# w1 and w2 laid out by 32x32 squares, so that VectorE instead of TensorE transposes them, in a fused kernel of attention approximation and NF4 feed-forward

## The chip, the cores and the metric

The kernel runs on one core of a Trainium2 chip. The metric is the device time of one execution in microseconds (us). The kernel before takes 429.08 us, the median of three runs (428.99 to 429.38).

## What is computed

For 1024 tokens x of width 512 the reference computes two layers. Each adds its result to x and normalises over the 512 features:

```
up = x @ up_w.T;  delta = x @ gate_w.T - local_point            # width 128
approx = sum over m = 0..6 of (term_m(delta) * up) @ W_m.T        # seven 128 -> 512 products
ffn1 = (silu(x @ ffn_gate_w.T) * (x @ ffn_up_w.T)) @ ffn_down_w.T # hidden width 1248
x = layernorm(x + approx + ffn1)
dq = nf4_quant_dequant(w)   # per 64 elements: a = max|w|; nearest of 16 codes to w/a; times a
ffn2 = (silu(x @ dq(w1).T) * (x @ dq(w2).T)) @ dq(w3).T           # hidden width 1376
x = layernorm(x + ffn2)
```

w1 and w2 are 1376 x 512 and w3 is 512 x 1376. All is float32.

## The kernel before, in words

**Products.** Each float32 product is three float32r matmuls over a high and a low part: `product()` issues hi·hi, lo·hi and hi·lo (L1144, L1145, L1146). The high part is a rounding copy made by ScalarE (`copy`, L557), the low part a subtraction on VectorE or GpSimd. So each operand passes through two engines before TensorE can read it.

**Stages on TensorE.** In order: `up` and `delta`; 20 pairs of the first layer's hidden projection; passes 0 and 1 of the first output stage (one for each half of the tokens); 22 pairs of the second layer's projection (`pair(2, i)`, 24 matmuls each, for hidden chunk f of 128 and one half of the tokens); passes 2 and 3 of the second output stage. The second layer's projection for chunk f needs the dequantised rows f of w1 and w2 with the contracted feature on the partitions. They come with the hidden row on the partitions, so `transpose_nf4(f)` turns them: eight 128x128 transposes (L1258) of the tile `Q` into PSUM banks 4 and 5. Two calls stand in pass 1 (f = 0, 1), one behind pair 2 and one behind each second pair after it (f = 2 to 10). ScalarE then copies both banks into one of two slots of `w_hi` (`split_nf4`), and VectorE subtracts into `w_lo` (`lo_nf4`, L915). `transpose_x` (L1244) and `transpose_w3` (L1269) do the same for x and w3 and stay.

**The NF4 work.** It runs beside all this on the other three engines, in 17 units: 0 to 10 are chunks of w1 and w2 (in the tile `Q`, 128 x 1024; unit 10 is 96 x 1024), 11 to 16 are thirds of w3 (in the tile `raw`, 128 x 896, the last ones 128 x 1024 in two parts). For a unit, VectorE takes the block maxima `amax` (L775), keeps them off zero and takes the reciprocal `rcp` (L781, L785), all three in `scales(u)`; GpSimd multiplies by `rcp` (L1060). Then come eight steps k: ScalarE draws a line through the unit and rounds it into an int8 tile `side` (L577 for k = 0, L557 after), GpSimd clamps that into a `level` (L1069, not for k = 0), and VectorE adds the level to a running sum in PSUM banks 6 and 7 (L796 for k = 1, L800 after). After k = 7 VectorE multiplies the sum by `amax` back into the unit (L807), and the unit is dequantised. There are four `side` and three `level` buffers, so GpSimd runs at most three levels ahead of VectorE's additions.

**What sets the order.** Every engine has one fixed program, written by hand. The NF4 steps stand in it where `beside()` is called: the table `SHARE` says for each call of each engine how many steps to take there. `SCALES_AHEAD` and `NORMALISE_AHEAD` put the scales and the multiplication a few steps ahead of a unit's first. Of the semaphores, `s_dq` counts dequantised units, `s_tr` transposed chunks, `s_wlo4` finished low parts. The two transposes of w3 behind the last pair (`transpose_w3(2)` and `(3)`) go into banks 6 and 7 and so wait for the last unit, 16.

**Elsewhere on GpSimd.** In passes 0 and 1 it makes the low parts of hidden activations (`l_lo`, L1099) and of the raw output weights (L1088), and in the second projection the product of gate and up (`h`, L1106), once for each pair.

Of the kernel before, what the change touches and what calls it, by code (L numbers as in the profile page):

```python
# [22 lines left out]
F32 = mybir.dt.float32  # L23
# [93 lines left out]

def unit_rows(u):
    return min(P, F2 - u * P) if u < C2 else P
# [12 lines left out]
def unit_width(u):  # L132
    return UW if u < C2 or is_last_third(u) else 2 * NARROW * BLOCK
# [13 lines left out]
def units_ahead(s, ahead):  # L147
    return [u for u in range(UNITS) if max(0, NB * u - ahead) == s]

# [59 lines left out]
def multiplied(i, pool):  # L209
# [20 lines left out]
    "gpsimd": [  # L230
# [15 lines left out]
def build(nc, xT, xN, w_pre, w_fuse, w_in, w_out, point, discount, w1, w2, w3, ident_in, out):  # L246
    with ExitStack() as ctx:
# [15 lines left out]
        amax, rcp = sb("amax", [P, 4, UW // BLOCK]), sb("rcp", [P, 2, UW // BLOCK])  # L263
# [17 lines left out]
        up2 = Q[:, 0, :].rearrange("p (i n) -> p i n", i=2)  # L281

# [36 lines left out]
        s_line0 = sem("s_line0")  # L319
        s_zero, s_warm = sem("s_zero"), sem("s_warm")  # L320
# [23 lines left out]
        s_xtr, s_tr, s_w3tr = sem("s_xtr"), sem("s_tr"), sem("s_w3tr")  # L344
        s_prep, s_nrm = sem("s_prep"), sem("s_nrm")
# [87 lines left out]
        NF4_BANK = 4  # L433
# [9 lines left out]
        def scaled(u):  # L443
            return 3 * unit_count(u)
# [6 lines left out]
        def unit_read(u):  # L451
            if u < C2:
                return Q[0:unit_rows(u), u, :]
# [8 lines left out]
        def unit_parts(u):  # L462
            p = unit_rows(u)
            if u < C2:
                return [(Q[0:p, u, :].rearrange("p (b e) -> p b e", e=BLOCK), 0, UW // BLOCK)]
# [8 lines left out]
        def per_block(t, u, b, n):  # L474
            v = t[0:unit_rows(u), u % t.shape[1], b:b + n]
            return v.rearrange("p (r b) -> p r b", r=2) if n == 2 * NARROW else v
# [16 lines left out]
        def _(sp):  # L493
# [13 lines left out]
            def load_unit(u):  # L507
                p = unit_rows(u)
                sp.dma_start(Q[0:p, u, 0:D], w1[u * P:u * P + p, :]).then_inc(s_q[u], 16)
                sp.dma_start(Q[0:p, u, D:2 * D], w2[u * P:u * P + p, :]).then_inc(s_q[u], 16)  # L510
# [44 lines left out]
        def _(act):  # L555
# [58 lines left out]
            def silu(layer, i):  # L614
# [8 lines left out]
                if layer == 2 and on_pool(i):  # L623
                    k = multiplied(i, True) - 1
                    if k == 0:

                        act.wait_ge(s_tr, 1)
                    elif k >= 2:
                        act.wait_ge(s_h2, k - 1)
# [16 lines left out]
            def split_x(t):  # L646
# [4 lines left out]
                else:  # L651
                    act.wait_ge(s_tile, TT)
                copy(x_hi[:, :, t * P:(t + 1) * P],
                     PS[:, NF4_BANK + t % 2, :].rearrange("p (c t) -> p c t", c=DC)).then_inc(s_xh, 1)

            def split_nf4(f):
                beside()
                m = rows(f, F2)
                act.wait_ge(s_tr, f + 1)
                wait_nf4_slot(act, f)  # L660
                copy(in_slot(w_hi, f, 2 * DC * m).rearrange("p (c m) -> p c m", m=m),
                     PS[:, NF4_BANK:NF4_BANK + 2, :].rearrange("p b (c m) -> p (b c) m", m=P)[:, :, 0:m]
                     ).then_inc(s_whi4, 1)
# [92 lines left out]
        def _(dve):  # L756
# [8 lines left out]
            def scales(u):  # L765
                p, done = unit_rows(u), scaled(u - 1)
                if u < C2:
                    dve.wait_ge(s_q[u], 32)
                else:
                    dve.wait_ge(s_w3[w3_place(u)[0]], 16)  # L770
                parts = unit_parts(u)
                if u >= 4:
                    dve.wait_ge(s_dq, quantised(u - 4))
                for blocks, b, n in parts:
                    v.tensor_reduce(per_block(amax, u, b, n), blocks, AX_X, ALU.max,  # L775
                                    apply_absolute_value=True).then_inc(s_prep, 1)
                if u >= 2:
                    dve.wait_ge(s_nrm, normalised(u - 2))
                for i, (_, b, n) in enumerate(parts):
                    dve.wait_ge(s_prep, done + i + 1)  # L780
                    v.tensor_scalar(rcp[0:p, u % 2, b:b + n], amax[0:p, u % 4, b:b + n], TINY, None,  # L781
                                    ALU.max).then_inc(s_prep, 1)
# [597 lines left out]
```

## Time and profile before

| what | value |
|---|---|
| median of three runs | 429.08 us |
| the profiled execution's own time | 429.23 us |
| its span, first to last instruction | 427.4 us |
| mean granted TensorE clock | 0.994 of full speed |
| TensorE (PE) busy | 417.5 us, 98% |
| VectorE (DVE) busy | 307.1 us, 72% |
| GpSimd (POOL) busy | 293.0 us, 69% |
| ScalarE (ACT) busy | 265.2 us, 62% |

The profile comes from one execution. A start is given in us from the start of the span. Matmuls are pipelined, so the distance between two starts, not the duration of one, is what a matmul costs the queue. Behind each group of instructions stands in brackets the idle time of its engine before it and what ended that. A share of busy time is an average over stages that have different limits.

### The profile page before, as it was taken

How to read it: one execution, taken by the hardware profiler on the slowest of the kernel's cores; microseconds unless marked ns; L12 is line 12 of the kernel's file. 1: busy time of each engine (PE TensorE's matmuls, PEld its weight loads, DVE VectorE, ACT ScalarE, POOL GpSimd, SP SyncE). 2: the span in 40 equal slices, each digit the busy share in tenths (PEclk: the TensorE clock that was granted, in tenths of full speed). 3: DMA queues.
4: the chain of work that ended last, by engine and by line, in shares of the span. 5: the costliest groups of instructions: out<-in, count | busy, mean ns of one | idle time of the engine just before them, and what ended most of it. 6: DMA issues, size and time to landing. Idle time of an engine off the chain costs nothing.

```text
span 427.4 us, 5638 instructions
## 1 busy us (share of the span) xinstructions
PE 417.5 (98%) x1908; PEld 342.9 (80%) x1908; DVE 307.1 (72%) x379; ACT 265.2 (62%) x356; POOL 293.0 (69%) x230
## 2 busy tenths in 40 slices
PE   8999999999999999999999999999999999999992
PEld 6888888888878888888878888888888877888881
DVE  3639989979879966978358889978699974216025
ACT  5576776677668554638837797788677864332612
POOL 0079999888784698248943788899989993444330
PEclk9999999999999999999999999999999999999997
DMA  8994110000013442020060000000000000000202
GB/s 266 399 352 157 51 38 25 26 25 26 25 49 107 145 141 72 0 100 1 0 265 1 2 0 2 0 2 0 2 2 0 2 0 0 2 0 2 98 0 99
DMA packets 10876, 26.51 MB, mean 62 GB/s; under 512 B 1472, under 2 KB 1728, under 8 KB 10336
## 3 DMA queue, kind: packets, MB, share of 16 engines
q1 hardware_dynamic: 10848, 26.16, 17.8%
q8 instruction: 15, 0.25, 0.2%
q14 instruction: 13, 0.11, 0.1%
HBM read 24.06 MB, written 2.10 MB: 61 GB/s over the span
## 4 chain that ended last, share of the span: by engine, by line
PE 88%; ACT 3%; DVE 3%; issue 2%; POOL 2%; DMA 1%; SPq 0%; ACTq 0%; POOLq 0%
PE PS L1144 28%; PE PS L1145 28%; PE PS L1146 28%; PE PS L1258 2%; DMA h<-xT 1%; PE PS L1269 1%; ACT x_hi L557 1%; ACT l_hi L557 1%; POOL x_lo L1088 1%; POOL l_lo L1099 1%; DVE std L894 1%; DVE stats L875 0%; ACT R L643 0%; DVE R L870 0%; PE PS L1244 0%
## 5 line engine op out<-in xcount | busy, mean ns | idle before, releaser
L1069 POOL TENSOR_SCALAR level<-side 128x1024 f32<-128x1024 int8 (+2 forms) x119 | 133.0, 1118 | 13.7 <-ACT side L557 4.1
L1144 PE MATMUL PS<-x_hi,w_hi 128*128 128x512 f32 (+1 forms) x352 | 138.4, 393 | 0.3 <-DVE x_lo L944 0.3
L1146 PE MATMUL PS<-x_hi,w_lo 128*128 128x512 f32 (+1 forms) x352 | 137.2, 390 | 0.0
L1145 PE MATMUL PS<-x_lo,w_hi 128*128 128x512 f32 (+1 forms) x352 | 137.1, 390 | 0.0
L800 DVE TENSOR_TENSOR PS<-PS,level 128x1024 f32<-128x1024 f32 (+2 forms) x102 | 121.8, 1194 | 19.6 <-POOL level L1069 15.1
L557 ACT ACTIVATE side<-Q 128x1024 int8<-128x1024 f32 (+1 forms) x77 | 77.5, 1050 | 16.9 <-DVE PS L796 11.0
L1099 POOL TENSOR_TENSOR l_lo<-h,l_hi 128x512 fp32r<-128x512 f32 (+1 forms) x42 | 55.9, 1337 | 46.4 <-ACT l_hi L557 45.9
L1144 PEld LDWEIGHTS PS<-x_hi,w_hi 128*128 128x128 f32 (+1 forms) x352 | 65.2, 185 | 15.0 <-issue 0.7
L1146 PEld LDWEIGHTS PS<-x_hi,w_lo 128*128 128x128 f32 (+1 forms) x352 | 65.2, 185 | 14.8
L1145 PEld LDWEIGHTS PS<-x_lo,w_hi 128*128 128x128 f32 (+1 forms) x352 | 65.3, 185 | 14.2
L1144 PE MATMUL PS<-x_hi,l_hi 128*128 128x512 f32 x144 | 56.8, 394 | 0.6 <-POOL l_lo L1099 0.6
L1146 PE MATMUL PS<-x_hi,l_lo 128*128 128x512 f32 x144 | 56.2, 390 | 0.0
L1145 PE MATMUL PS<-x_lo,l_hi 128*128 128x512 f32 x144 | 56.1, 390 | 0.0
L622 ACT ACTIVATE h<-PS 128x512 f32<-128x512 f32 (+1 forms) x42 | 25.0, 595 | 41.8 <-PE PS L1146 41.5
L1088 POOL TENSOR_TENSOR w_lo<-raw,w_hi 128x1024 fp32r<-128x1024 f32 (+2 forms) x15 | 31.3, 2090 | 23.6 <-ACT w_hi L557 23.0
L557 ACT ACTIVATE l_hi<-h 128x512 fp32r<-128x512 f32 (+1 forms) x42 | 25.9, 625 | 26.0 <-PE PS L1146 26.0
L557 ACT ACTIVATE side<-raw 128x896 int8<-128x896 f32 (+1 forms) x42 | 38.8, 986 | 3.9 <-DVE PS L796 3.7
L1106 POOL TENSOR_TENSOR h<-h,Q 128x512 f32<-128x512 f32 (+1 forms) x22 | 30.0, 1368 | 6.9 <-ACT Q L557 4.5
L1060 POOL TENSOR_TENSOR Q<-Q,rcp 128x1024 f32<-128x1024 f32 (+1 forms) x11 | 21.0, 1905 | 17.2 <-DVE rcp L785 17.1
L1144 PEld LDWEIGHTS PS<-x_hi,l_hi 128*128 128x128 f32 x144 | 27.1, 188 | 6.2 <-issue 0.8
L1146 PEld LDWEIGHTS PS<-x_hi,l_lo 128*128 128x128 f32 x144 | 27.0, 188 | 5.7
L1144 PE MATMUL PS<-w_hi,l_hi 128*128 128x512 f32 (+1 forms) x80 | 31.6, 395 | 0.0
(77 smaller groups left out, 518.9 us busy)
## 6 DMA issues: line engine op xcount, KB each, us to landing
Q<-w SPq DMA_DIRECT2D x20, 256.0 KB, 9.8
raw<-w_in SPq DMA_DIRECT2D x9, 512.0 KB, 9.7
raw<-w_out SPq DMA_DIRECT2D x14, 256.0 KB, 2.6
raw<-w SPq DMA_DIRECT2D x2, 1376.0 KB, 7.8
R<-xN SPq DMA_DIRECT2D x2, 1024.0 KB, 5.1
out<-R SPq DMA_DIRECT2D x8, 256.0 KB, 2.0
raw<-w_fuse SPq DMA_DIRECT2D x7, 256.0 KB, 2.6
h<-xT SPq DMA_DIRECT2D x3, 512.0 KB, 6.9
```

The lines of the kernel that those rows point to most:

```text
L557: return nc.scalar.activation(dst, src, ACT.Copy, **kw)
L622: nc.scalar.activation(dst, PS[0:dst.shape[0], bank, :], ACT.Silu).then_inc(s_silu, 1)
L800: v.tensor_tensor(total, total, level_of(s), ALU.add).then_inc(s_add, 1)
L1060: g.tensor_tensor(blocks, blocks, spread(rcp, u, b0, n), ALU.mult).then_inc(s_nrm, 1)
L1069: g.tensor_scalar(level_of(s), side_of(s), LIMITS[k][1], LIMITS[k][0], ALU.min, ALU.max).then_inc(s_level, 1)
L1088: g.tensor_tensor(lo, w_raw(j)[0:p, 0:n], hi.bitcast(F32), ALU.subtract).then_inc(s_wlo_in if JOBS[j][0] == "in" else s_wlo, 1)
L1099: g.tensor_tensor(lo, view, hi.bitcast(F32), ALU.subtract).then_inc(s_llo_h, 1)
L1106: g.tensor_tensor(dst, dst, up2[0:dst.shape[0], k % 2, :], ALU.mult).then_inc(s_h2, 1)
L1144: t_.matmul(dst, a_hi, b_hi, start=start, stop=False)
L1145: t_.matmul(dst, a_hi, b_lo, start=False, stop=False)
L1146: return t_.matmul(dst, a_lo, b_hi, start=False, stop=stop)
L1258: last = t_.transpose(PS[:, NF4_BANK + g_, c * P:c * P + m], Q[0:m, f, g_ * D + c * P:g_ * D + (c + 1) * P], ident[0:m, 0:m])
```

## The change

**Layout.** The host lays w1 and w2 out together as `w12`, in squares of 32: on partition p a unit now holds 32x32 squares such that transposing each square alone, in place, gives the matrix that TensorE wants. The 512 features are also permuted (`order`) in x, the output weights and w3, and back in the result. Unit 10 becomes 128 x 768 where it was 96 x 1024. `w12` is loaded with one DMA for each unit where there were two.

**Transposes.** `transpose_nf4` is gone from TensorE. VectorE gets `turn_nf4(f)`: one instruction, 128 x 1024 (128 x 768 for f = 10), from `Q` into banks 4 and 5, in runs of 32 that alternate between the banks. It stands one chunk earlier than TensorE's did: `turn_nf4(f + 3)` follows `lo_nf4(f + 2)`. The copy and the subtraction stay, and now read a contiguous piece.

**Scales.** `scales(group)` makes the scales of unit 0, then of two units together (1 and 2, up to 15 and 16): the maxima unit by unit, but one instruction each for keeping them off zero and for the reciprocal. `amax` has six slots, `rcp` four.

**Steps.** All three lists of `SHARE` are new.

```diff
+SCALE_GROUPS = [range(0, 1)] + [range(u, u + 2) for u in range(1, UNITS, 2)]
...
 SHARE = {
     "scalar": [
-        0, 0, 0, 4, 0, 4, 2, 0, 2, 0, 3, 0, 0, 3, 0, 2, 0, 1, 4, 0, 3, 2, 0, 3, 3, 0, 2, 4, 0, 2, 3, 0, 3, 0,
+        0, 0, 0, 4, 2, 2, 1, 0, 3, 0, 2, 0, 0, 2, 1, 3, 0, 1, 3, 0, 4, 2, 0, 3, 3, 0, 4, 2, 0, 2, 5, 0, 3, 0,
...
             def load_unit(u):
-                p = unit_rows(u)
-                sp.dma_start(Q[0:p, u, 0:D], w1[u * P:u * P + p, :]).then_inc(s_q[u], 16)
-                sp.dma_start(Q[0:p, u, D:2 * D], w2[u * P:u * P + p, :]).then_inc(s_q[u], 16)
+                sp.dma_start(unit_read(u), w12[:, u * UW:u * UW + unit_width(u)]).then_inc(s_q[u], 16)
...
+            def scales(group):
+                if group[-1] >= 6:
+                    dve.wait_ge(s_dq, quantised(group[-1] - 6))
+                for u in group:
...
+                    for blocks, b, n in unit_parts(u):
+                        v.tensor_reduce(per_block(amax, u, b, n), blocks, AX_X, ALU.max,
+                                        apply_absolute_value=True).then_inc(s_max, 1)
+                dve.wait_ge(s_max, unit_count(group[-1]))
...
+                v.tensor_scalar(inverse, maxima, TINY, None, ALU.max).then_inc(s_floor, 1)
+                dve.wait_ge(s_floor, scaled(group[-1]))
+                v.reciprocal(inverse, inverse).then_inc(s_prep, 1)
...
+            def turn_nf4(f):
+                beside()
+                dve.wait_ge(s_dq, quantised(f))
+
+                if f in (0, 2):
+                    dve.wait_ge(s_xl, X_PARTS + (TILES if f == 0 else TT))
+                else:
+                    dve.wait_ge(s_wlo4, f)
+                v.transpose(turned(f).rearrange("p (s n i) -> p n s i", s=2, i=SQ),
+                            unit_read(f).rearrange("p (n s j) -> p n s j", s=2, j=SQ)).then_inc(s_turn, 1)
...
                 if i == 2:
                     lo_nf4(2)
+                    turn_nf4(3)
                 elif half == 1 and f + 2 < C2:
                     lo_nf4(f + 2)
+                    if f + 3 < C2:
+                        turn_nf4(f + 3)
...
-            def transpose_nf4(f):
-                m = rows(f, F2)
-                pe.wait_ge(s_dq, quantised(f))
...
-                for g_ in range(2):
-                    for c in range(DC):
-                        last = t_.transpose(PS[:, NF4_BANK + g_, c * P:c * P + m],
-                                            Q[0:m, f, g_ * D + c * P:g_ * D + (c + 1) * P], ident[0:m, 0:m])
-                last.then_inc(s_tr, 1)
```

**The order on GpSimd** from the end of pass 1 to the third pair of the second projection. Before (L1099 is `l_lo`, L1069 a level, L1060 the multiplication by `rcp`, L1106 gate times up):

```order
L1088 TENSOR_TENSOR x_lo<-raw,x_hi 128x512
L1069 TENSOR_SCALAR level<-side 128x1024
L1099 TENSOR_TENSOR l_lo<-h,l_hi 128x512
L1069 TENSOR_SCALAR level<-side 128x1024 x2
L1060 TENSOR_TENSOR Q<-Q,rcp 128x1024
L1069 TENSOR_SCALAR level<-side 128x1024
L1106 TENSOR_TENSOR h<-h,Q 128x512
L1069 TENSOR_SCALAR level<-side 128x1024 x3
L1106 TENSOR_TENSOR h<-h,Q 128x512
```

With the change (the same four are L1133, L1103, L1094 and L1140):

```order
L1122 TENSOR_TENSOR x_lo<-raw,x_hi 128x512
L1133 TENSOR_TENSOR l_lo<-h,l_hi 128x512
L1094 TENSOR_TENSOR Q<-Q,rcp 128x1024
L1103 TENSOR_SCALAR level<-side 128x1024 x6
L1140 TENSOR_TENSOR h<-h,Q 128x512
L1103 TENSOR_SCALAR level<-side 128x1024
L1094 TENSOR_TENSOR Q<-Q,rcp 128x768
L1103 TENSOR_SCALAR level<-side 128x1024
L1140 TENSOR_TENSOR h<-h,Q 128x512
```

The level ahead of the last `l_lo` is gone from there, and unit 9's multiplication and three more levels stand ahead of the first gate times up.

**The order on VectorE** in the middle of the second projection, before (L915 is the low part of a chunk of w1 and w2):

```order
L807 TENSOR_TENSOR raw<-PS,amax 128x2x448
L915 TENSOR_TENSOR w_lo<-PS,w_hi 128x1024
L796 SCALAR_TENSOR_TENSOR PS<-side,level 128x896
L800 TENSOR_TENSOR PS<-PS,level 128x896
L775 TENSOR_REDUCE amax<-raw 128x14
L781 TENSOR_SCALAR rcp<-amax 128x14
L785 RECIPROCAL rcp<-rcp 128x14
L800 TENSOR_TENSOR PS<-PS,level 128x896 x5
```

With the change (L940 is that low part, L931 the transpose, L812 an addition):

```order
L940 TENSOR_TENSOR w_lo<-PS,w_hi 128x1024
L812 TENSOR_TENSOR PS<-PS,level 128x896
L819 TENSOR_TENSOR raw<-PS,amax 128x2x448
L931 STREAM_TRANSPOSE PS<-Q 128x16x2x32
L808 SCALAR_TENSOR_TENSOR PS<-side,level 128x896
L812 TENSOR_TENSOR PS<-PS,level 128x896
L788 TENSOR_REDUCE amax<-raw 128x14 x2
L795 TENSOR_SCALAR rcp<-amax 128x32
L797 RECIPROCAL rcp<-rcp 128x32
L812 TENSOR_TENSOR PS<-PS,level 128x896 x3
```

A transpose has come in for each chunk, and the small instructions for the scales stand once for two units.

## Rows read from the trace of the kernel before

**Rows 1.** Page, busy us of each engine (share of the span), instructions:

```profile
PE 417.5 (98%) x1908; PEld 342.9 (80%) x1908; DVE 307.1 (72%) x379; ACT 265.2 (62%) x356; POOL 293.0 (69%) x230
```

**Rows 2.** Waits of PE: line, releaser, us in total, times, longest:

```profile
PE PS L1276 <- POOL level L1109: 1.2, 1, 1.2
PE PS L1144 <- POOL l_lo L1099: 0.6, 1, 0.6
PE PS L1144 <- DVE x_lo L944: 0.3, 1, 0.3
```

**Rows 3.** Chain of waits, f = 2 and f = 10 of nine pieces: start, us, what:

```profile
242.95 0.87 PE PS L1258 x8
...
331.70 0.66 PE PS L1258 x8
```

**Rows 4.** Timeline of PE at the end of pass 1 (f = 1):

```profile
214.70 1.03 PE L1258 MATMUL PS<-ident,Q 128*128 128x128 f32 x8
216.37 0.47 PE L1144 MATMUL PS<-x_hi,l_hi 128*128 128x512 f32 x1 [0.63 <-POOL l_lo L1099]
216.67 0.40 PE L1145 MATMUL PS<-x_lo,l_hi 128*128 128x512 f32 x1
216.91 0.40 PE L1146 MATMUL PS<-x_hi,l_lo 128*128 128x512 f32 x1
```

**Rows 5.** Timeline of POOL around the start of the second projection:

```profile
213.82 1.04 POOL L1069 TENSOR_SCALAR level<-side 128x1024 f32<-128x1024 int8 x1
214.94 1.28 POOL L1099 TENSOR_TENSOR l_lo<-h,l_hi 128x512 fp32r<-128x512 f32 x1
216.30 2.17 POOL L1069 TENSOR_SCALAR level<-side 128x1024 f32<-128x1024 int8 x2
230.66 1.90 POOL L1060 TENSOR_TENSOR Q<-Q,rcp 128x1024 f32<-128x1024 f32 x1 [12.19 <-DVE rcp L785]
234.37 1.28 POOL L1106 TENSOR_TENSOR h<-h,Q 128x512 f32<-128x512 f32 x1 [0.68 <-ACT Q L557]
```

**Rows 6.** Timelines at the last pair: POOL, then DVE, then PE:

```profile
347.19 4.41 POOL L1069 TENSOR_SCALAR level<-side 128x1024 f32<-128x1024 int8 x4
...
353.94 1.22 DVE L807 TENSOR_TENSOR raw<-PS,amax 128x448 f32<-128x448 f32 x2
...
355.22 1.09 PE L1269 MATMUL PS<-ident,raw 128*128 128x128 f32 x8
```

**Rows 7.** Busy us (instructions) by stretch: PE, PEld, DVE, ACT, POOL, clock, DMA, GB/s:

```profile
228.80:355.30 126.50, 126.50 (x608) 104.01 (x607) 108.97 (x118) 96.62 (x127) 109.87 (x93) 1.00 0.00 1
230.70:351.60 120.90, 120.90 (x581) 100.06 (x580) 103.55 (x109) 95.10 (x125) 108.53 (x92) 1.00 0.00 1
```

**Rows 8.** Groups by line and shape: busy us, mean ns, idle before:

```profile
L1069 POOL TENSOR_SCALAR level<-side 128x1024 f32<-128x1024 int8 x84 | 97.0, 1155 | 10.6 <-ACT side L557 3.8 <-DVE PS L800 0.6
L1069 POOL TENSOR_SCALAR level<-side 128x896 f32<-128x896 int8 x28 | 28.7, 1026 | 2.6 <-ACT side L557 0.4
L800 DVE TENSOR_TENSOR PS<-PS,level 128x1024 f32<-128x1024 f32 x72 | 88.2, 1225 | 13.2 <-POOL level L1069 10.3
L800 DVE TENSOR_TENSOR PS<-PS,level 128x896 f32<-128x896 f32 x24 | 26.3, 1094 | 5.7 <-POOL level L1069 4.4
L775 DVE TENSOR_REDUCE amax<-Q 128x16 f32<-128x1024 f32 x10 | 12.1, 1211 | 0.0
L781 DVE TENSOR_SCALAR rcp<-amax 128x16 f32<-128x16 f32 x10 | 4.5, 448 | 0.9
L785 DVE RECIPROCAL rcp<-rcp 128x16 f32<-128x16 f32 x10 | 2.5, 253 | 0.3
L964 DVE SCALAR_TENSOR_TENSOR R<-R 128x1024 f32<-128x1024 f32 x1 | 2.1, 2092 | 0.0
```

**Rows 9.** Timelines for chunk 5: its low part on DVE, then the pair that needs it:

```profile
276.71 1.21 DVE L915 TENSOR_TENSOR w_lo<-PS,w_hi 128x1024 fp32r<-128x1024 f32 x1
...
285.23 0.48 PE L1144 MATMUL PS<-x_hi,w_hi 128*128 128x512 f32 x1
```

More of the change, by code:

```diff
@@ L243, in job_rows, with build @@
     return P if kind == "fuse" else rows(f, F1) if kind == "out" else rows(f, F2)
-def build(nc, xT, xN, w_pre, w_fuse, w_in, w_out, point, discount, w1, w2, w3, ident_in, out):
+def build(nc, xT, xN, w_pre, w_fuse, w_in, w_out, point, discount, w12, w3, ident_in, out):
     with ExitStack() as ctx:
@@ L281, in build, with turned @@
         up2 = Q[:, 0, :].rearrange("p (i n) -> p i n", i=2)
+        def turned(f):
+            return PS[:, XT_BANK:XT_BANK + 2, :].rearrange("p b n -> p (b n)")[:, 0:unit_width(f)]
         def term_tile(m, a):
@@ L443, in scaled @@
         def scaled(u):
-            return 3 * unit_count(u)
+            return [u in group for group in SCALE_GROUPS].index(True) + 1
         normalised = quantised = unit_count
@@ L810, in add_step @@
                 for u in units_ahead(s, SCALES_AHEAD):
-                    scales(u)
+                    for group in SCALE_GROUPS:
+                        if u == group[0]:
+                            scales(group)
                 if STEPS[s][1] > 0:
@@ L1314, in _ @@
                     transpose_x(TILES + 1)
-                elif i == 2:
-                    transpose_nf4(2)
-                elif half == 1 and f + 2 < C2:
-                    transpose_nf4(f + 2)
                 elif (f, half) == (C2 - 1, 0):
@@ L1352, in chunks_in, with by_squares @@
         return np.ascontiguousarray(np.concatenate(parts, axis=1))
+    def by_squares(*ws):
+        parts = []
+        for f in range(C2):
+            rows_ = [w[f * P:(f + 1) * P].reshape(-1, SQ, 2, DC, BLOCK) for w in ws]
+            parts.append(np.stack(rows_).transpose(4, 2, 0, 3, 1, 5).reshape(P, -1))
+        return np.ascontiguousarray(np.concatenate(parts, axis=1))
+    order = np.arange(D).reshape(2, DC, 2, SQ).transpose(0, 2, 1, 3).reshape(D)
     x = a(L0_attn_hidden_states)
@@ L1358 @@
         "xT": np.ascontiguousarray(x2.T.reshape(DC, P, TOK).transpose(1, 0, 2)),
-        "xN": np.ascontiguousarray(x2.reshape(TT, P, D).transpose(1, 0, 2)),
+        "xN": np.ascontiguousarray(x2[:, order].reshape(TT, P, D).transpose(1, 0, 2)),
         "w_pre": np.ascontiguousarray(chunks_in(a(L0_attn_up_w), a(L0_attn_gate_w)).reshape(P, 2, DC, P)
@@ L1362 @@
         "w_fuse": np.ascontiguousarray(np.stack([a(L0_attn_local_approx_output).T]
-                                                + [fuse[:, :, g].T for g in range(G)])),
+                                                + [fuse[:, :, g].T for g in range(G)])[:, :, order]),
         "w_in": chunks_in(a(L0_attn_ffn_gate_w), a(L0_attn_ffn_up_w)),
-        "w_out": np.ascontiguousarray(a(L0_attn_ffn_down_w).T),
+        "w_out": np.ascontiguousarray(a(L0_attn_ffn_down_w).T[:, order]),
         "point": a(L0_attn_local_point).reshape(S, 1),
         "discount": a(L0_attn_discount_factor).reshape(1, G),
-        "w1": np.ascontiguousarray(a(L0_ffn_w1)),
-        "w2": np.ascontiguousarray(a(L0_ffn_w2)),
-        "w3": np.ascontiguousarray(a(L0_ffn_w3)).reshape(D // 2, PAIR),
+        "w12": by_squares(a(L0_ffn_w1), a(L0_ffn_w2)),
+        "w3": np.ascontiguousarray(a(L0_ffn_w3)[order]).reshape(D // 2, PAIR),
         "ident_in": np.eye(P, dtype=np.float32),
@@ L1378 @@
     r = run_bass_kernel_spmd(nc, [arrays], core_ids=[0])
-    return r.results[0]["out"].reshape(x.shape)
+    return r.results[0]["out"][:, np.argsort(order)].reshape(x.shape)
```

106 lines of the change are left out of this document (47 added, 59 removed), and 19 rows, old and new, of the table SHARE.

## The prediction

> **What bounds the kernel now.** I read the page first: TensorE is busy 98% of the span, the next engine 72% [rows 1]. The waits of PE confirm it: three waits, 2.1 us together, of which two (1.2 and 0.3) belong to the start, ahead of the warm-up and of the first products, and one of 0.6 is for `l_lo` [rows 2]. So what leaves TensorE's queue leaves the kernel's time, as long as the operands still come in time. The rest of the reading is about that condition, and two places matter. At the end of pass 1 TensorE is not its own limit: it finishes the transposes that start at 214.70 and then waits 0.63 for an `l_lo` of GpSimd [rows 4]. At the last pair of the second projection the NF4 work is just in time: GpSimd's last four levels end at 351.60, VectorE's last multiplications at 355.16, and TensorE starts the transposes that need them at 355.22 [rows 6]. Between those two places GpSimd is busy 108.53 of 120.90 us and VectorE 108.97 of 126.50 [rows 7]. TensorE leads by nothing there: whatever it gains, the NF4 work must gain too, or the gain turns into a wait at 355.
>
> **Term 1, transposes in the second projection: 7.6 us.** Nine groups of eight go (f = 2 to 10). The chain of waits has them as nine pieces, eight of 0.87 and a narrow one of 0.66 [rows 3]: 8 x 0.87 + 0.66 = 7.6. They lie in the chain one after the other with matmuls on both sides, so they count in full.
>
> **Term 2, transposes in pass 1: 1.6 us, between 1.1 and 2.5.** Two groups go here (f = 0, 1). Without them TensorE would be ready at 214.70 - 0.87 = 213.83 in place of 216.37, a gain of 2.5. But it needs the last `l_lo`, which GpSimd starts at 214.94, right behind a level that started at 213.82 [rows 5]. The new order takes this level from there, so the `l_lo` can start at 213.82, which is 1.1 earlier. That is the sure part. How much faster the engines get through the stretch before it (three fewer lines on ScalarE, no multiplication by `rcp` in GpSimd's way) the trace doesn't show. I take 1.6, nearer the low end, since the low end is a row and the high end only TensorE's own limit.
>
> **Edits at nothing.** The copies and subtractions of the turned chunk keep their sizes. One DMA in place of two for a unit saves SyncE's queue time while nothing waits for it, and `x`, the first thing that TensorE waits for, is queued ahead of them. The paired scales and the steps dealt anew in the first projection put up to six additions (6 x 1.225 = 7.4 us [rows 8]) between two of VectorE's gate products. TensorE has three pairs of banks there and so bears a lag of two pairs, 2 x 24 matmuls that start 0.24 apart at most [rows 4], 11 us. If that cover failed, each microsecond of lag beyond it would be paid once. The weights of chunk f have a lead: the low part of chunk 5 starts at 276.71, ends at 277.92, and is read from 285.23 on [rows 9]. The transpose on VectorE comes one chunk earlier than the one on TensorE did, so this lead of 7.3 us shrinks only by what VectorE's queue is late.
>
> **Sum.** 7.6 + 1.6 = 9.2. Against the profiled execution's own 429.23 that is 420.0; its time is 0.15 above the median, so the median should be 419.9. TensorE would reach the last transposes at 355.22 - 9.2 = 346.0.
>
> **What the transpose costs on VectorE.** No row shows one. The nearest rows are 1024 wide, with one operand in SBUF: the maxima, 1.211, and an addition into PSUM, 1.225 [rows 8]. I take 1.22 (0.96 for the narrow unit 10). Below: nothing, if it were hidden, still only helps an engine that isn't the limit. Above: the slowest 1024-wide instruction of VectorE, 2.092, with two operands in SBUF [rows 8]; the transpose has one.
> The Trainium skill speaks against the change here: by VectorE: DVE Perf Modes, The three transpose paths, a 128x128 bf16 transpose takes 311 ns on VectorE, and the same page's Rules for kernel authors give a transpose of 128x128 to TensorE where PSUM will do as the target. As an estimate from that page alone, eight of them would be 2.5 us for a unit and the sum would be some 425. Against it the Vector Engine (DVE) Microarchitecture Reference, The reshape front-end and per-opcode configuration, says the array sustains one element per cycle per lane; by that rule one long instruction costs like the maxima row, and the sum stays. No row here shows which.
>
> **Does VectorE keep up?** From the end of the second group of normalisations (228.8 before) to the last multiplication it was busy 108.97. Leave out the scales of units 9 and 10, now made in pass 1: 2 x (1.21 + 0.45 + 0.25) = 3.8. Leave out four additions of unit 8, now made between the normalisations: 4.9. Unit 10 is 256 narrower, 1.02 ns per element from the two addition rows, eight instructions: 2.1. Eight pairs of small instructions for units 11 to 16 become three, 5 x 0.70 = 3.5, of which I count 3, as the new ones are wider. Add nine transposes, 8 x 1.22 + 0.96 = 10.7. That makes 105.9. The time for it runs from about 228.1 (1.6 earlier, 0.9 later for the addition that stands in the normalisation) to 346.0: 117.9 us. So 12 us may be idle, where 17.5 were.
>
> **Does GpSimd keep up?** It had 12.19 us of idle time ahead of unit 9's multiplication, waiting for `rcp`, which VectorE could make only behind the normalisations [rows 5]. Now the scales of 9 and 10 are there long before, and this multiplication and six levels, not none, fill that gap (two ran before it in both): 1.90 + 6 x 1.155 = 8.8 us less to do later. The narrow unit 10 saves about 1.4 more. From 108.53 that leaves 98.3. It starts with the first gate times up, 234.37 - 1.6 = 232.8, and ended 12.4 us of idle and gaps later than its busy time says; 3.0 of these were waits for `rcp` of one unit, which the pairs should end. So the last level ends at 232.8 + 98.3 + 9.4 = 340.5, or 343.5 if no wait goes. It must end 3.6 before TensorE's arrival, at 342.4, and one subtraction of 0.7 no longer stands behind it. The margin is 2.6 us, and -0.4 at the other end. This is thin, and it is where I expect an error.
>
> **Rivals.**
> (a) *The NF4 work is late at the last pair.* For it: the margin above, VectorE at 90% with transposes that its additions queue behind, and a buffer of only three levels between two engines that are now both nearly full. Against it: both balances close. TensorE would wait 1 to 4 us at the transposes of w3: 421 to 424.
> (b) *A transpose costs 2.1 us,* the upper bound above. VectorE's busy time grows by 9 x 0.87 = 7.8 us, to 113.7 of 117.9. That leaves 4.2 us of idle time; if 5 to 9 can't be avoided (half of the 17.5 before, when GpSimd was the slower engine, is 9), the last unit is late by 1 to 5 us: 421 to 425. For it: the write alternates between two banks in runs of 32, which no row shows. Against it: only one operand lies in SBUF.
> The Trainium skill's table of the three transpose paths would make this some 425, as said above.
> (c) *Slower: VectorE becomes the bound.* If each 32x32 square paid a fixed cost like that of VectorE's smallest instruction here, 0.253 for 16 elements [rows 8], 32 squares would take 8.1 us. The point from which this decides: the 9.2 gained and about 7 us of spare time on VectorE are used up by nine transposes at (9.2 + 7)/9 = 1.8 above 1.2, so 3.0 us each. At 4 us the kernel would take 419.9 + 9 x 2.8 - 7 = 438, at 8.1 some 475. Against it: nothing in the long instructions here hints at a cost by the run.
> (d) *No change.* TensorE's freed time is lost again because another engine paces the second projection already. The rows of waits speak against it: there is none in that stretch [rows 2].
>
> **How the numbers follow.** The forecast (419.0 to 420.9, from term 2's bounds and a wait below 1 us) has 0.62, (a) 0.25, (b) 0.07, (c) 0.03, (d) 0.03. A measurement of this kernel can tell some 0.2%, 0.9 us, from no change. Faster is the forecast with (a) and (b), 0.94; within 0.2% is (d), 0.03; slower is (c), 0.03. The range goes down to 418.9, term 2 at its high end with a little to spare, and up to 424.0, all of (a) and most of (b); outside are (c), (d) and the end of (b).
>
> **What would show it.** Right: no L1258-like group on PE, 1820 matmuls in place of 1908; no idle of PE from the second projection to the transposes of w3, which start near 346; transposes near 1.22 on VectorE, nine of them in that stretch; GpSimd's last level ending near 340 to 342, and no 12 us gap before unit 9; the matmul behind pass 1's last `l_lo` 1.1 to 2.5 earlier than 216.37. Wrong: an idle time before the transposes of w3 released by VectorE's last multiplication (a); VectorE busy over 112 us in that stretch (b, c); a span shorter by less than 8 us without such a wait would mean that term 1 isn't paid by the queue.

## The result and the profile after

The change makes the kernel **faster**: 418.89 us (median of four runs, 418.46 to 419.06) against 429.23 (four runs, 428.99 to 429.41), a ratio of 0.9758 with a 95% interval of 0.9741 to 0.9775. The profiled execution took 419.06 against 429.23, its span 417.2 against 427.4. The forecast was 419.9, in a range of 418.9 to 424.0. The measured median lies 1.0 below the forecast and 0.01 below the range.

The page of the kernel after, in the form of [rows 1]:

```profile
PE 408.3 (98%) x1820; PEld 334.0 (80%) x1820; DVE 314.2 (75%) x371; ACT 263.9 (63%) x356; POOL 291.3 (70%) x230
```

There are 88 matmuls fewer (11 groups of 8) and TensorE is still busy 98% of a shorter span. Its waits after, as in [rows 2], and below them the one of its weight loads that matters:

```profile
PE PS L1298 <- POOL level L1143: 1.2, 1, 1.2
PE PS L1178 <- POOL l_lo L1133: 0.2, 1, 0.2
PE PS L1178 <- DVE x_lo L970: 0.2, 1, 0.2
...
PEld PS L1291 <- DVE raw L819: 0.3, 1, 0.3
```

The first row is the start again. The 0.6 for the last `l_lo` has gone; the 0.2 is a new wait, for a different `l_lo`, at the start of pass 1. The last row is the transposes of w3, which wait 0.3 for VectorE's last multiplication (0.4 before).

The new instruction on VectorE (count, shortest/median/longest in ns, first and last start, forms):

```profile
L931 DVE STREAM_TRANSPOSE PS<-Q x11: 983/1250/1260, 208.5 to 324.0; 128x1024 f32<-128x1024 f32 x10, 128x768 f32<-128x768 f32 x1
```

The timelines of the kernel after at the end of pass 1 and the start of the second projection (PE, then POOL), and at the last pair (POOL, DVE, PE). They answer to [rows 4], [rows 5] and [rows 6]:

```profile
214.51 0.47 PE L1178 MATMUL PS<-x_hi,l_hi 128*128 128x512 f32 x1
...
213.08 1.29 POOL L1133 TENSOR_TENSOR l_lo<-h,l_hi 128x512 fp32r<-128x512 f32 x1
214.33 1.90 POOL L1094 TENSOR_TENSOR Q<-Q,rcp 128x1024 f32<-128x1024 f32 x1
216.31 4.41 POOL L1103 TENSOR_SCALAR level<-side 128x1024 f32<-128x1024 int8 x4
222.66 1.04 POOL L1103 TENSOR_SCALAR level<-side 128x1024 f32<-128x1024 int8 x1 [1.93 <-DVE PS L812]
229.52 1.05 POOL L1103 TENSOR_SCALAR level<-side 128x1024 f32<-128x1024 int8 x1 [5.82 <-DVE PS L812]
...
337.74 4.41 POOL L1103 TENSOR_SCALAR level<-side 128x1024 f32<-128x1024 int8 x4
...
344.10 1.22 DVE L819 TENSOR_TENSOR raw<-PS,amax 128x448 f32<-128x448 f32 x2
...
345.38 1.09 PE L1291 MATMUL PS<-ident,raw 128*128 128x128 f32 x8
```

The last `l_lo` starts at 213.08 in place of 214.94, and the matmul behind it at 214.51 with no wait, in place of 216.37. GpSimd's gap of 12.19 before unit 9 is gone; two gaps of 1.93 and 5.82 are left, in which it waits for VectorE's additions. At the last pair the three engines meet within about a microsecond again: GpSimd's last level ends at 342.15, VectorE's last multiplications at 345.32, and TensorE starts at 345.38.

The windows of the kernel after, as [rows 7] (the first for VectorE's balance, the second for GpSimd's):

```profile
228.00:345.40 117.40, 117.40 (x531) 95.85 (x529) 105.32 (x107) 90.91 (x123) 99.68 (x87) 1.00 0.00 1
232.80:342.20 109.40, 109.40 (x492) 89.78 (x490) 97.53 (x97) 86.38 (x117) 97.34 (x85) 1.00 0.00 1
```

**Where the time went.** The starts of the same matmuls, before minus after, give the gain as it grows along the queue:

| where | before | after | gain so far |
|---|---|---|---|
| first product | 6.79 | 7.08 | -0.29 |
| last matmul of pass 0 | 168.10 | 168.29 | -0.2 |
| first matmul of pass 1 | 168.32 | 168.87 | -0.55 |
| behind the last `l_lo` of pass 1 | 216.37 | 214.51 | 1.86 |
| behind the first group gone from the second projection | 243.58 | 240.90 | 2.68 |
| behind the second | 249.91 | 246.34 | 3.57 |
| behind the ninth | 332.14 | 322.50 | 9.64 |
| last matmul | 419.29 | 409.46 | 9.83 |
| end of the span | 427.4 | 417.2 | 10.2 |

Pass 1 gives 1.86 + 0.55 = 2.41. The second projection gives 9.64 - 1.86 = 7.78. Another 0.19 comes behind that, half of it from the ninth group still, and 0.4 between the last matmul and the end of the span.

Two small losses stand ahead of pass 1. The kernel after is 0.2 late from its start; in the eight kernels of experiments 1 to 4 that are made from the kernel after the first matmul behind TensorE's second wait comes anywhere between 9.64 and 10.85 (10.20 before, 10.38 after), so these 0.2 can't be put down to the change. The wait of 0.2 for an `l_lo` costs 0.35 more. All eight kernels with the new steps lose it at this place, and the two of experiment 1, with the old lists, don't: it is a price of the new steps.

The 0.4 at the end lies behind the last computation. ScalarE's last instruction, before and then after, is still 9.83 apart, as the last matmul is:

```profile
423.11 0.81 ACT L643 ACTIVATE R<-R,std 128x512 f32<-128x512 f32 x1 [1.02 <-DVE std L896]
...
413.28 0.81 ACT L659 ACTIVATE R<-R,std 128x512 f32<-128x512 f32 x1 [1.01 <-DVE std L910]
```

It is no chance of one execution. From the start of the last matmul to the end of the span it takes 7.7 in all ten traces of kernels with the new layout, whatever their steps, and 8.1 in all three with the old one. What makes it is open.

### The profile page after: what moved, and what is told of

Read it like the earlier page. It is cut to its first block, busy times and chain, and to the rows that moved or that the text cites. A ratio compares the mean times of both kernels' runs of the same rounds, so it can differ in the third digit from the quotient of the medians.

```text
span 417.2 us, 5429 instructions
## 1 busy us (share of the span) xinstructions
PE 408.3 (98%) x1820; PEld 334.0 (80%) x1820; DVE 314.2 (75%) x371; ACT 263.9 (63%) x356; POOL 291.3 (70%) x230
## 4 chain that ended last, share of the span: by engine, by line
PE 91%; POOL 2%; DVE 2%; DMA 2%; issue 1%; ACT 0%; SPq 0%; POOLq 0%
PE PS L1178 30%; PE PS L1180 30%; PE PS L1179 30%; DMA h<-xT 2%; POOL l_lo L1133 1%; PE PS L1291 1%; PE PS L1281 1%; POOL level L1103 1%; DVE stats L889 1%; DVE R L884 0%; ACT R L659 0%; DVE x_lo L970 0%; ACT x_hi L573 0%; DVE mv L898 0%; SPq L537 0%
## 5 line engine op out<-in xcount | busy, mean ns | idle before, releaser
L1103 POOL TENSOR_SCALAR level<-side 128x1024 f32<-128x1024 int8 (+2 forms) x119 | 130.0, 1092 | 29.3 <-DVE PS L812 12.1
L812 DVE TENSOR_TENSOR PS<-PS,level 128x1024 f32<-128x1024 f32 (+2 forms) x102 | 120.3, 1179 | 21.5 <-POOL level L1103 16.8
L573 ACT ACTIVATE side<-Q 128x1024 int8<-128x1024 f32 (+1 forms) x77 | 76.5, 1031 | 18.6 <-DVE PS L808 9.7
L1133 POOL TENSOR_TENSOR l_lo<-h,l_hi 128x512 fp32r<-128x512 f32 (+1 forms) x42 | 58.3, 1396 | 38.5 <-ACT l_hi L573 38.0
L1140 POOL TENSOR_TENSOR h<-h,Q 128x512 f32<-128x512 f32 (+1 forms) x22 | 29.4, 1335 | 8.7 <-ACT Q L573 7.4
L1179 PEld LDWEIGHTS PS<-x_lo,l_hi 128*128 128x128 f32 x144 | 27.1, 188 | 5.4
```

The source lines that it names most:

```text
L573: return nc.scalar.activation(dst, src, ACT.Copy, **kw)
L812: v.tensor_tensor(total, total, level_of(s), ALU.add).then_inc(s_add, 1)
L1103: g.tensor_scalar(level_of(s), side_of(s), LIMITS[k][1], LIMITS[k][0], ALU.min, ALU.max).then_inc(s_level, 1)
L1133: g.tensor_tensor(lo, view, hi.bitcast(F32), ALU.subtract).then_inc(s_llo_h, 1)
L1140: g.tensor_tensor(dst, dst, up2[0:dst.shape[0], k % 2, :], ALU.mult).then_inc(s_h2, 1)
L1179: t_.matmul(dst, a_hi, b_lo, start=False, stop=False)
```

## The experiments

### 1. The transposes moved, the steps as before

The kernel after, but with the lists of `SHARE` of the kernel before; in the first of the two the scales are also made unit by unit. In both, `turn_nf4` doesn't call `beside()`, so that the old lists fit the calls.

```diff
-SCALE_GROUPS = [range(0, 1)] + [range(u, u + 2) for u in range(1, UNITS, 2)]
+SCALE_GROUPS = [range(u, u + 1) for u in range(UNITS)]
...
             def turn_nf4(f):
-                beside()
                 dve.wait_ge(s_dq, quantised(f))
```

> The changed kernel with the steps of the kernel before and scales unit by unit: only the layout and the transposes on VectorE are new. Theory N (the NF4 work must gain as much as TensorE): GpSimd's program is the old one, its gap of 12 us before unit 9 stays, only the narrow unit 10 makes it 1.4 us shorter, and VectorE has 10.7 us more to do. The last unit is done at 353 to 358 us, TensorE waits 7 to 12 us for it at the transposes of w3, and the time is 427 to 431 us. Theory Q (what leaves TensorE's queue leaves the time, whatever the steps): 419 to 421 us, no wait above 1 us.

**Measured:** 435.01 us (434.3 to 436.77), ratio to before 1.0137 (1.0107 to 1.0167): slower than the kernel before, and above the 427 to 431 that my own theory expected. The waits of PE:

```profile
PE PS L1176 <- ACT Q L572: 5.1, 6, 1.7
PE PS L1289 <- DVE raw L818: 3.9, 1, 3.9
PE PS L1176 <- POOL l_lo L1131: 2.4, 1, 2.4
```

Its PE timeline behind the wait at the end of pass 1, GpSimd's two instructions ahead of it, and PE at the transposes of w3:

```profile
216.08 0.47 PE L1176 MATMUL PS<-x_hi,l_hi 128*128 128x512 f32 x1 [2.44 <-POOL l_lo L1131]
...
217.44 0.63 PE L1177 MATMUL PS<-x_lo,l_hi 128*128 128x512 f32 x1
217.86 0.63 PE L1178 MATMUL PS<-x_hi,l_lo 128*128 128x512 f32 x1
...
213.55 1.04 POOL L1101 TENSOR_SCALAR level<-side 128x1024 f32<-128x1024 int8 x1
214.67 1.27 POOL L1131 TENSOR_TENSOR l_lo<-h,l_hi 128x512 fp32r<-128x512 f32 x1
...
360.50 1.97 PE L1289 MATMUL PS<-ident,raw 128*128 128x128 f32 x8 [3.85 <-DVE raw L818]
```

The windows of the stretch behind the first of these waits:

```profile
216.00:220.30 4.30, 4.22 (x12) 3.35 (x13) 1.65 (x2) 1.65 (x2) 2.08 (x2) 0.60 1.00 424
```

**What follows.** The level still stands ahead of the last `l_lo`, so TensorE, which arrives early, only waits longer: term 2 is nothing (216.08 against 216.37, and this run is 0.3 ahead from its start). In the second projection the gates' copies on ScalarE (`Q`, made just before GpSimd's product) come late six times, and the last unit is late by 3.9. And there is a loss on top that no balance of mine held: behind the waits of 2.44 and 3.85 the granted clock was low (0.60 over 216.0 to 220.3), and the matmuls started 0.43 apart, not 0.23. That is the lower level, 1.2 GHz in place of 2.4. By the starts, the first of these stretches costs eight matmuls 0.2 each, 1.6 in all; the second, where eight transposes take 1.97 in place of 1.09, costs 1.4.

> The same with the scales of two units made together, still the steps of before. Theory N: the waits of GpSimd for rcp of a single unit (3.0 us between 248 and 320) go, the gap of 12 us stays: the last unit is done some 3 us earlier than in the run with the turns alone, time 424 to 428 us. Theory Q: 419 to 421 us, as with the turns alone.

**Measured:** 434.63 us (434.38 to 436.13), ratio 1.0132 (1.0114 to 1.015). This misses the 424 to 428 that I expected: the paired scales alone change nothing that can be told apart (the ranges of the two kernels overlap). TensorE waits 6.8 in five waits for `Q`, 3.0 for the last unit and 2.4 for the `l_lo`. So it is the lists that matter.

### 2. The steps and scales as after, the transposes on TensorE

```diff
             def turn_nf4(f):
                 beside()
-                dve.wait_ge(s_dq, quantised(f))
...
-                v.transpose(turned(f).rearrange("p (s n i) -> p n s i", s=2, i=SQ),
...
+            def transpose_nf4(f):
...
+                for c in range(unit_width(f) // P):
+                    last = t_.transpose(turned(f)[:, c * P:(c + 1) * P], Q[:, f, c * P:(c + 1) * P], ident[:])
```

> The changed kernel (layout, paired scales, new steps) with the transposes back on TensorE, of the new layout, so w_hi holds wrongly arranged weights. Both theories: TensorE's queue is as full as before. It gains only the 0.6 us that it waited for l_lo at the end of pass 1 and the 0.4 at the last unit: 428 to 429.3 us. If it comes out at 426 or less, the steps save something on TensorE's path that the reading missed.

**Measured:** 428.32 us (median of seven; six lie between 427.76 and 428.35, one took 469.92), ratio 0.9974 (0.9963 to 0.9986), as expected. Its matmul behind the last `l_lo`, without a wait:

```profile
215.57 0.48 PE L1170 MATMUL PS<-x_hi,l_hi 128*128 128x512 f32 x1
```

**What follows.** With experiment 1 this makes a square: nothing 429.2, the steps and scales alone 428.3, the transposes alone 435.0, both 418.9. (All but the first have the new layout, and with it the 0.4 at the end.) The two parts don't add. TensorE's 9.4 us (428.32 - 418.89) are there only where the other three engines have been dealt their steps anew, and without that the same move costs 5.8. The redeal is worth 0.9 where TensorE keeps its transposes and some 16 where it doesn't.

### 3. What pays at the end of pass 1

Three kernels move one instruction each. Each ran once, and single runs of one kernel differ by more than half a microsecond here (428.87 to 429.59 for the kernel before), so the readings go by places in the traces and not by the totals. The first is the kernel before with the level moved from ahead of the last `l_lo` to behind it (`SHARE`, "gpsimd", calls 42 and 43: 1, 3 become 0, 4).

> The kernel before with one level moved on GpSimd from ahead of the last l_lo of pass 1 to behind it, nothing else. Theory N: the wait of 0.63 us at 216.37 goes, TensorE is 0.6 us ahead from there, and waits that much longer for the last unit at the transposes of w3 (355): time unchanged within 0.3 us. Rival (TensorE's time ahead is kept): 0.6 us shorter at the end, no longer wait at 355.

**Measured:** 428.0 in one run beside 428.77 for the kernel before on the same chip. The PE timeline behind the last `l_lo`, and GpSimd at unit 9's multiplication:

```profile
215.18 0.48 PE L1127 MATMUL PS<-x_hi,l_hi 128*128 128x512 f32 x1
...
229.44 1.90 POOL L1043 TENSOR_TENSOR Q<-Q,rcp 128x1024 f32<-128x1024 f32 x1 [11.38 <-DVE rcp L768]
```

The matmul starts 1.19 earlier than in [rows 4], some 0.3 of which this run already has from its start, and TensorE does not wait. The last matmul is still 1.21 earlier, so the gain is not lost at the last unit: unit 9's multiplication also comes 1.2 earlier (229.44 against 230.66), because the second projection's work begins from the end of pass 1. So the theory that GpSimd's work hangs on a fixed balance and eats any early gain has fallen, and the reading behind term 2 holds.

The second is the kernel before with unit 8's multiplication one step later, so that a level stands ahead of it in the first normalisation:

```diff
-                for u in units_ahead(s, NORMALISE_AHEAD):
+                for u in [x for x in range(UNITS) if max(0, NB * x - (2 if x == 8 else NORMALISE_AHEAD)) == s]:
```

> The kernel before with unit 8's multiplication by rcp one step later on GpSimd, so that it doesn't run beside VectorE's small instructions of the first normalisation. Theory P (two instructions that each read two operands of SBUF hold each other up): the instruction L894, 1.83 us beside the multiplication, takes 1.1 or less, the chain from the root to the first normalised tile is 0.7 us or more shorter, and GpSimd's l_lo's start so much earlier. Rival (it was slow for another reason): L894 stays above 1.5.

**Measured:** 428.41 in one run beside 428.77. The place it is about is VectorE's short chain on 128 x 4 elements that makes the factors of the normalisation. In the kernel before, DVE and then POOL:

```profile
190.41 0.18 DVE L892 RECIPROCAL std<-std 128x4 f32<-128x4 f32 x1 [1.98 <-ACT std L636]
191.01 1.83 DVE L894 SCALAR_TENSOR_TENSOR std<-std 128x4 f32<-128x4 f32 x1
193.07 0.89 DVE L896 SCALAR_TENSOR_TENSOR std<-mv,std 128x4 f32<-128x4 f32 x1
...
190.91 1.90 POOL L1060 TENSOR_TENSOR Q<-Q,rcp 128x1024 f32<-128x1024 f32 x1
192.90 2.17 POOL L1069 TENSOR_SCALAR level<-side 128x1024 f32<-128x1024 int8 x2
```

With the multiplication later, DVE, POOL, and PE at the end of pass 1:

```profile
191.02 0.16 DVE L894 SCALAR_TENSOR_TENSOR std<-std 128x4 f32<-128x4 f32 x1
191.22 0.89 DVE L895 SCALAR_TENSOR_TENSOR std<-std 128x4 f32<-128x4 f32 x1
...
191.06 1.04 POOL L1069 TENSOR_SCALAR level<-side 128x1024 f32<-128x1024 int8 x1
192.18 1.91 POOL L1060 TENSOR_TENSOR Q<-Q,rcp 128x1024 f32<-128x1024 f32 x1
...
215.51 0.48 PE L1144 MATMUL PS<-x_hi,l_hi 128*128 128x512 f32 x1
```

In the kernel after, DVE and POOL:

```profile
191.57 0.16 DVE L906 RECIPROCAL std<-std 128x4 f32<-128x4 f32 x1
191.97 0.92 DVE L908 SCALAR_TENSOR_TENSOR std<-std 128x4 f32<-128x4 f32 x1
193.12 0.16 DVE L910 SCALAR_TENSOR_TENSOR std<-mv,std 128x4 f32<-128x4 f32 x1
...
191.84 1.04 POOL L1103 TENSOR_SCALAR level<-side 128x1024 f32<-128x1024 int8 x1
```

**What follows.** The instruction of line 894 takes 1.83 beside GpSimd's multiplication and 0.16 without it. In all three kernels the long one of VectorE's small instructions ends as GpSimd's ends: 192.84 and 192.81, 192.11 and 192.10, 192.89 and 192.88. The chain from the reciprocal to its end takes 3.55 before (190.41 to 193.96) and 1.71 after (191.57 to 193.28). In the kernel after it begins later, since an addition stands ahead of it, so it ends 0.68 earlier; with the 1.12 of the level that is 1.8 of the 1.86 by which the last `l_lo` is earlier. And the multiplication's move alone was enough to take away the wait for the last `l_lo` (215.51 against 216.37). So the new steps have two gains in pass 1, and my term 2 counted one. Each alone removes the whole wait that the kernel before shows, so they don't add there. That both are needed once TensorE arrives another transposes' length earlier is worked out from these rows; no run that has the transposes moved has just one of the two.

The third is the kernel after with a level put back ahead of the last `l_lo` ("gpsimd", calls 42 and 43: 0, 7 become 1, 6).

> The changed kernel with that level put back ahead of the last l_lo. If the level was the sure part of term 2, the matmul behind pass 1's last l_lo starts 1.0 to 1.2 us later than 214.51; the 0.3 us wait for the last unit then goes, so the whole loses 0.7 to 0.9 us. If the rest of the queue absorbs it, less than 0.3 us.

**Measured:** 423.45 in one run, 4.6 above the kernel after and not 0.7 to 0.9. POOL, then PE:

```profile
212.75 1.91 POOL L1076 TENSOR_TENSOR Q<-Q,rcp 128x1024 f32<-128x1024 f32 x1
214.75 1.04 POOL L1085 TENSOR_SCALAR level<-side 128x1024 f32<-128x1024 int8 x1
215.87 1.27 POOL L1115 TENSOR_TENSOR l_lo<-h,l_hi 128x512 fp32r<-128x512 f32 x1
...
217.29 0.61 PE L1160 MATMUL PS<-x_hi,l_hi 128*128 128x512 f32 x1 [2.98 <-POOL l_lo L1115]
```

and the windows behind it:

```profile
217.20:221.40 4.20, 4.11 (x11) 3.31 (x12) 0.12 (x1) 2.32 (x3) 2.08 (x2) 0.59 0.92 387
```

**What follows.** I had overlooked that in the new lists this level is the third ahead of unit 9, and so carries unit 9's multiplication with it: the `l_lo` starts 2.8 later, not 1.1. TensorE waits 2.98, and the clock is low again behind the wait (0.59), which stretches nine starts by 0.2, another 1.7. Together that is 4.7, against 4.6 measured. As a measurement of the level alone this run fails. As one of what a wait costs here it is the clearest.

### 4. How much room VectorE and GpSimd had left

The kernel after with every transpose on VectorE issued twice in a row:

```diff
+                v.transpose(turned(f).rearrange("p (s n i) -> p n s i", s=2, i=SQ),
+                            unit_read(f).rearrange("p (n s j) -> p n s j", s=2, j=SQ)).then_inc(s_twice, 1)
+                dve.wait_ge(s_twice, f + 1)
```

> The changed kernel with each transpose on VectorE made twice, one behind the other: what a transpose of 2.5 us would cost. It adds 9 x 1.25 = 11 us to VectorE between 228 and 345, where it was busy 105.3 of 117.4. Theory N with the prediction's reckoning for a dear transpose (part of the idle time can't be used): the last unit is 4 to 9 us late, 423 to 428 us. Theory Q, or idle time that can all be used: within 1 us of the changed kernel's 418.9.

**Measured:** 427.56 us (427.04 to 428.79), ratio 0.9964 (0.9952 to 0.9975). Waits of PE, and the window of the second projection up to its later end:

```profile
PE PS L1182 <- issue: 4.6, 3, 3.6
PE PS L1182 <- ACT Q L574: 1.6, 2, 1.3
```

```profile
228.00:354.00 126.00, 119.39 (x535) 95.92 (x534) 118.67 (x121) 90.40 (x125) 98.96 (x87) 1.00 0.00 1
```

**What follows.** Nine more transposes of 1.26 put 11.3 us on VectorE in the second projection, where it was idle for 117.4 - 105.3 = 12.1. The kernel pays 8.7 of the 11.3. So only 2.6 of the 12.1 idle microseconds could be used in this order; the others lie where VectorE has nothing it may do. The starts of the matmuls show 0.6 lost at 236 and the rest coming in steps from 290 on, the greatest at the first pair of chunk 9, whose low part VectorE ends at 329.86; TensorE waits 3.6 there and starts at 329.96. Rival (c) took about 7 us of spare time as usable. By this slope the change would break even near 1.26 + 1.26 x 10.3/8.7 = 2.75 us for a transpose, an estimate from the two kernels, and not at 3.0.

The kernel after without the second matmul of each `product()` in pairs 18 and 19 (the high part of w12 times the low part of x), 16 matmuls or 3.6 us less for TensorE just before the last unit:

```diff
-                t_.matmul(dst, a_hi, b_lo, start=False, stop=False)
+                if not light[0]:
+                    t_.matmul(dst, a_hi, b_lo, start=False, stop=False)
```

> The changed kernel with 16 matmuls left out: of the pairs 18 and 19 of the second projection the product hi x lo of x isn't made. TensorE's queue is 16 x 0.227 = 3.6 us shorter, just ahead of the transposes of w3. Theory N: the last unit is still done at 345, TensorE waits some 3.9 us for it (0.3 before), time within 0.5 us of the changed kernel's. Theory Q: 3.6 us shorter, 415.3 us.

**Measured:** 419.88 us (419.01 to 420.22), ratio 0.9776 (0.9762 to 0.9791): 1.0 above the kernel after, though TensorE has 3.6 less to do. The wait and the window behind it:

```profile
PE PS L1180 <- ACT Q L573: 3.3, 1, 3.3
```

```profile
333.08:337.08 4.00, 4.00 (x11) 2.66 (x12) 2.97 (x3) 2.93 (x4) 3.84 (x3) 0.57 0.00 0
```

**What follows.** What TensorE gains before the last unit it loses whole to a wait, as I expected, but in another place: two pairs earlier, for ScalarE's copy of a gate product, and not at the transposes of w3. VectorE's last multiplications start at 343.94 and hold nobody up. The clock behind the wait is low (0.57) with no DMA running beside it; eight matmuls are stretched by 0.2 each there, 1.5 in all, and 3.3 + 1.5 is more than the 3.6 saved.

Two more kernels give GpSimd less: its clamps for units 15 and 16 are half as wide, once together with the lighter pairs and once alone.

```diff
-                    g.tensor_scalar(level_of(s), side_of(s), LIMITS[k][1], LIMITS[k][0], ALU.min,
+                    w = 512 if STEPS[s][0] >= UNITS - 2 else unit_width(STEPS[s][0])
+                    g.tensor_scalar(level_of(s)[:, 0:w], side_of(s)[:, 0:w], LIMITS[k][1], LIMITS[k][0], ALU.min,
```

> The same, and GpSimd clamps only half the width of units 15 and 16 (512 of 1024 elements, 14 levels), so that the NF4 work should end 3 to 7 us earlier. Theory N: now TensorE's 3.6 us come through, with the 0.3 of the wait: 415.0 us. If the time stays at 418 to 419 although the NF4 work ends earlier, something else holds TensorE.

> The changed kernel with only the half-width clamps of units 15 and 16, TensorE's queue whole. Theory N and Q alike: the wait of 0.3 us goes, no more: 418.5 us. It bounds what a shorter NF4 chain alone is worth now.

**Measured:** together 417.43 us (416.67 to 419.7), ratio 0.973 (0.9694 to 0.9766); the clamps alone 418.68 (418.15 to 418.75), ratio 0.9749 (0.9734 to 0.9763). The wait of PE where both are in:

```profile
PE PS L1181 <- DVE w_lo L940: 1.9, 1, 1.9
```

**What follows.** The clamps alone give nothing that can be told from the kernel after, as expected: TensorE can't go faster. Together with the lighter pairs the median is 1.5 lower, where I had expected the whole 3.6. The four runs scatter widely, and their range overlaps that of the kernel after; but the trace bears the size out, since 3.6 less a wait of 1.9 is 1.7. TensorE then waits for the low part of chunk 10 on VectorE. So with GpSimd out of the way VectorE is next, 1.9 behind. The forecast's margin of 2.6 for GpSimd is not there on any of the three engines.

### 5. The start

The kernel after with VectorE's memset of `amax` behind the first low parts.

> The changed kernel with the new memset of amax put behind the first low parts on VectorE. If it is what made TensorE start 0.3 us later (7.08 against 6.79), the first product starts at 6.8 again. Where the last unit sets the pace at the transposes of w3, the end gains less than 0.3 us.

**Measured:** 418.91 in one run, against 418.89: nothing. The first product does start at 6.86 in place of 7.08, but this proves little. In the eight kernels of experiments 1 to 4 that are made from the kernel after, with the memset where it was, it starts anywhere from 6.08 to 7.61. What sets the start stays open.

No kernel here that computes everything beats the kernel after. The only ones below it leave work out.

## Why the prediction was right or wrong

**The bound and its condition: right.** What leaves TensorE's queue leaves the time, if the operands come. Removing the 11 groups is worth 9.4 between experiment 2 and the kernel after. Experiments 1 and 4 show the condition, as it fails.

**Term 1, 7.6: right in kind, 0.2 to 0.3 small.** The starts give 7.78, 0.89 for a full group (3.57 - 2.68) where I took 0.87 from the chain of waits. A group costs a little more than its piece of the chain: it puts off the next matmul by 0.80, and the one behind that by 0.09 more (243.58 and 243.89 before, 240.90 and 241.13 after).

**Term 2, 1.6 between 1.1 and 2.5: the step that failed, by its size.** Pass 1 gives 2.41, nearly the end that I had called TensorE's own limit: both groups of transposes and the whole wait of 0.63 are gone. At the matmul that I named the gain is 1.86, because 0.55 was lost ahead of pass 1. I took a value near the low end because the level was a row and the rest was not. The rest was in the trace all the same. The `l_lo` starts 1.86 earlier, 1.1 of it by the level; I had named "no multiplication by `rcp` in GpSimd's way" without pricing it. Its own row, 1.90, stands right beside a 1.83 of VectorE on 512 elements, and that pair of rows would have moved the value to the high end.

**The sum and the range.** 420.0 was forecast for the profiled execution, 419.06 came. The difference of 1.0 is 0.8 in term 2, 0.2 in term 1, 0.2 behind the second projection, 0.4 behind the last matmul, less the 0.55 ahead of pass 1. So beside term 2 a second thing was missing, a term for the end of the program, which I had at nothing without a reason. The low end of the range held term 2's high end with nearly nothing for the small terms, each of a few tenths, and the result went past it by 0.01. That last step over the edge is chance, since the four runs differ by 0.6; the error of 1.0 is not.

**The edits at nothing: right but for one.** No new wait for weights, gates or DMAs stands among the waits of PE. But the steps dealt anew bring the one for an `l_lo` at the start of pass 1, which costs 0.35. I had looked only at their effect on the first projection.

**The transpose at 1.22: right, 1.25.** The narrow one takes 983 ns (0.96 taken); the 256 columns between them cost 267 ns, 1.04 ns each. By the table in the Trainium skill's VectorE: DVE Perf Modes, The three transpose paths, eight would have been 2.5 us, an estimate that the trace does not bear out for one long instruction. By the rule in the Trainium skill's Vector Engine (DVE) Microarchitecture Reference, The reshape front-end and per-opcode configuration, the array sustains one element per cycle per lane. The trace agrees so far as it can: 1.04 ns for a further column is the 1.02 of the additions, within 2%.

**VectorE's balance: right.** 105.9 forecast, 105.32 in the window of 117.4. What I drew from it was too much: 12 us idle, of which rival (c) took about 7 as usable. Experiment 4 finds 2.6.

**GpSimd's balance: the busy time right, its end late.** 98.3 forecast, 97.34 measured. But the last level ends at 342.15, not 340.5, still inside the 343.5 that I named. I had counted the gap before unit 9 as filled; 7.75 us of it came back as waits for VectorE's additions, since only three levels fit between the two. The margin of 2.6 before TensorE was in truth none: the weights of the w3 transposes wait 0.3. It came out as no loss because all three arrive together, though TensorE came 0.6 earlier than the 346.0 forecast. That is luck: nothing in my reckoning held the three so close.

**The rivals.** (a), the NF4 work late, is what happens with the old lists (3.9 at that place) and the kernel after stands 0.3 from it. (b) is refuted by the row of the transpose. (c) too, though its point of decision was set too far off. (d) is refuted by the 7.78. A rival that I did not have is the one that experiment 1 brought: a wait costs more than its length, since the clock can fall behind it.

## What to carry to other kernels

Taking work off the bounding engine pays in full only as far as the others are just as far ahead: count the change and the redealing of the others' work as one, since here either alone was worth -5.8 and +0.9 and both together +10.3. Idle time in a balance is not room; test it by doubling the added instruction. Where a row is far too long for its size, look which instruction of another engine ends with it.

## What the hardware showed that I had not expected

**A small instruction of VectorE waits for one of GpSimd.** On 128 x 4 elements in SBUF, 0.16 became 1.83, 0.89 or 0.92, each time until the GpSimd instruction beside it ended (experiment 3). The Trainium skill, SBUF — State Buffer, SBUF: two separate sides, says that the two share a pair of ports, which one of them holds for a whole instruction where VectorE has two inputs in SBUF and GpSimd reads SBUF; the rows agree with it. Larger instructions may pay too: in the kernel after, VectorE's first addition of a unit, with `side` and `level` both in SBUF, takes 1.51 in the mean on 1024 columns, and the later ones, with one operand there, 1.23. That this is the same effect is not shown.

**The clock can fall behind a single wait.** TensorE's granted clock was 0.57 to 0.60 over some 4 us behind waits of 2.44, 2.98 and 3.3, with matmuls 0.43 apart in place of 0.23 for eight or nine of them. It was 1.00 on both sides of that. It fell behind the waits for the last unit in experiment 1 too (3.85 and 3.03), where TensorE went on with transposes. It did not fall behind the waits of 1.9 and 1.3, nor each time behind long ones: in the doubled transposes 3.58 us of idle time leave it at full speed:

```profile
329.96 0.47 PE L1182 MATMUL PS<-x_hi,w_hi 128*128 128x512 f32 x1 [3.58 <-issue]
330.26 0.40 PE L1183 MATMUL PS<-x_lo,w_hi 128*128 128x512 f32 x1
```

and so does the wait of 2.44 at the end of pass 1 in the second kernel of experiment 1, whose windows row behind it is

```profile
216.90:221.00 4.10, 4.06 (x18) 3.39 (x19) 1.92 (x2) 1.60 (x2) 2.07 (x2) 1.00 1.01 428
```

What tells these cases apart is open. Where it falls, a wait of 3 us costs nearly 5.
